# A block of binary convolutions and a mixture of 16 experts on one core: the operands of the up product exchanged, token weights put on the down product, odd pages' down product in float32

## What is computed

```
t = t + ffn(ln_t(t))                               # tokens of 64 values
logits = x @ gate_w + gate_b                       # 16 experts, the best 2 are kept
dispatch = their probabilities, scaled to sum 1
hidden = silu(x @ w1[e]) * (x @ w2[e])             # 64 -> 128 for each chosen expert
out    = sum over chosen e of dispatch[e] * (hidden @ w3[e])   # 128 -> 64
```

## Time and profile before

| | |
|---|---|
| times of three runs | 538.88, 543.08, 543.24 us; median 543.08 |
| span of the profiled execution, first to last instruction | 598.9 us, 14226 instructions |
| TensorE, matmuls | 500.9 us, 84% of the span |
| VectorE | 441.6 us, 74% |
| ScalarE | 396.0 us, 66% |
| GpSimd | 287.9 us, 48% |
| granted TensorE clock, mean | 0.901 |
| chain that ended last | PE 51%, DVE 17%, ACT 10%, issue 9% |

### The profile page before, as it was taken

How to read it: one execution, slowest core, us unless ns; L and a number is a source line. 1 busy time by engine, 2 the same in 40 slices (tenths; PEclk the granted TensorE clock), 3 DMA queues, 4 the chain that set the end, 5 groups by cost and what they waited for, 6 DMA issues and landing times.

```text
span 598.9 us, 14226 instructions
## 1 busy us (share of the span) xinstructions
PE 500.9 (84%) x4186; PEld 436.7 (73%) x4186; DVE 441.6 (74%) x1242; ACT 396.0 (66%) x946; POOL 287.9 (48%) x378
## 2 busy tenths in 40 slices
PE   6899997896986627767889899999999999999854
PEld 5566665674764516757878799999998999899753
DVE  4567786685689697556676688888888888888653
ACT  5577885684765303456676588888787878778650
POOL 4000036666667675645555455454444544545351
PEclk9878997996979557879999899999999999999986
DMA  7941101011000012320122221232242425210404
GB/s 295 283 84 36 35 12 61 25 60 62 25 24 29 22 46 66 69 63 21 39 56 57 54 43 39 51 90 54 48 116 49 118 55 147 55 31 17 134 24 141
DMA packets 62664, 40.97 MB, mean 68 GB/s; under 512 B 50003, under 2 KB 54318, under 8 KB 62080
## 3 DMA queue, kind: packets, MB, share of 16 engines
q1 hardware_dynamic: 52208, 23.84, 17.5%
q0 software_dynamic: 8800, 8.94, 4.4%
q10 hardware_dynamic: 1584, 7.29, 3.2%
HBM read 21.46 MB, written 19.19 MB: 68 GB/s over the span
## 4 chain that ended last, share of the span: by engine, by line
PE 51%; DVE 17%; ACT 10%; issue 9%; another core or an unknown queue 6%; DMA 4%; SPq 3%; POOLq 0%; DVEq 0%; ACTq 0%; POOL 0%
PE up L971 9%; PE up L973 8%; PE turn L987 6%; PE up L803 5%; PE lines L1004 5%; PE small L819 3%; ACT xc L703 3%; DVE hidden L1589 2%; DMA x_in<-in_x 2%; PE lines L1006 2%; PE small L848 2%; PE up L789 2%; PE small L952 2%; PE up L778 2%
## 5 line engine op out<-in xcount | busy, mean ns | idle before, releaser
L519 POOL DMA_INDIRECT results<-result,page_in x147 | 154.3, 1050 | 152.0 <-ACT xc L703 103.5
L498 POOL DMA_INDIRECT pages<-payload,slot_int x128 | 127.6, 997 | 141.7 <-DVE slot_int L1414 73.5
L971 PE MATMUL up<-up_w,xs_hi 128*128 x588 | 163.5, 310 | 9.8 <-issue 5.1
L973 PE MATMUL up<-up_w,xs_lo 128*128 x588 | 150.0, 287 | 0.3 <-issue 0.3
L703 ACT ACTIVATE xc<-up 128x512 f32<-128x512 f32 x147 | 89.5, 609 | 76.5 <-PE up L973 48.4
L971 PEld LDWEIGHTS up<-up_w,xs_hi 128*128 128x128 f32 x588 | 114.1, 194 | 16.2 <-issue 13.7
L973 PEld LDWEIGHTS up<-up_w,xs_lo 128*128 128x128 f32 x588 | 114.7, 195 | 0.0
L1589 DVE SCALAR_TENSOR_TENSOR hidden<-up,page_in,xc 128x128 f32<-128x128 f32 x196 | 59.4, 344 | 43.2 <-ACT xc L703 35.4
L1599 DVE TENSOR_TENSOR hidden_lo<-turn,hidden_hi 128x512 f16<-128x512 f32 x98 | 67.0, 684 | 3.9 <-ACT hidden_hi L716 2.8
L987 PE MATMUL turn<-ident,hidden 128*128 128x128 f32 x392 | 60.7, 279 | 2.8 <-DVE branch L1599 1.6
L716 ACT ACTIVATE hidden_hi<-turn 128x512 f16<-128x512 f32 x98 | 60.9, 622 | 3.1 <-PE turn L987 2.5
(11 more groups left out here) (262 smaller groups left out, 999.2 us busy)
## 6 DMA issues: line engine op xcount, KB each, us to landing
pages<-up_w ACTq DMA_DIRECT2D x4, 1332.0 KB, 9.9
page_in<-pages SPq DMA_DIRECT2D x147, 36.0 KB
page_in<-pages SPq DMA_DIRECT2D x147, 32.0 KB
x_in<-in_x SPq DMA_DIRECT2D x7, 512.0 KB
out<-up_raw SPq DMA_DIRECT2D x5, 512.0 KB, 4.8
results<-result,page_in POOLq DMA_INDIRECT x147
up_raw<-in_L_ffn_w SPq DMA_DIRECT2D x4, 512.0 KB, 16.8
pages<-payload,slot_int POOLq DMA_INDIRECT x128
```

The costliest lines, as they stand in the source:

```text
L498: pool.indirect_dma_start(out=pages, out_offset=bass.IndirectOffsetOnAxis(ap=slot_int[q % PAYLOADS][:, t:t + 1], axis=0), in_=payload[q % ...
L519: pool.indirect_dma_start(out=results, out_offset=bass.IndirectOffsetOnAxis(ap=page_in[g % LOADS][:, k, D + AT_TOKEN:D + AT_TOKEN + 1].bit ...
L971: pe.matmul(target, xs_hi[g % 2][:, k * P:(k + 1) * P], weights[:, bass.ds(e * 2, 2 * HID)], start=True, stop=False)
L973: last = pe.matmul(target, xs_lo[g % 2][:, k * P:(k + 1) * P], weights[:, bass.ds(e * 2, 2 * HID)], start=False, stop=True)
```

## The change

- The up product exchanges its operands: an expert's 128 columns of `up_w` are stationary (gate or value, each apart) and the page's 128 tokens move, `xs_hi` and `xs_lo` one after the other. The result has hidden units in partitions, gates in the first bank and values in the second, each with its own semaphore. `up_w`, `xs_hi` and `xs_lo` are float16, with scales.
- So `turn_hidden` goes. `hide` is one operation on VectorE over all four experts, without the tokens' weights. ScalarE has the silu alone, and `hidden_high` from SBUF for even pages.
- The down product of each expert goes to a place of its own, two pages in one bank of `turn`. Even pages have three float16 matmuls for each expert; odd pages one in float32, from `hidden` and `down_raw`, which is scaled in place.
- VectorE multiplies the down product of two pages by the tokens' weights (`weigh`), and GpSimd sums the four experts of a group in two additions (`sum_up`, called between its scatters by `sums_behind`); for the last two groups VectorE does it (`tail_sum`).
- `LAG` is 3 in place of 4, hidden rows have 4 buffers, and `turn_back` writes to `lines`. `make_hi(0)` and `make_low(0)` move to later steps of the first stage, and the blank page lies in the last three pairs of `x2`.

```diff
-    LAG = 4
-    SCALED = 2
+    LAG = 3
+    RING = 4
...
-        up_w = sb("up_w", [P, E, 2, HID], F32R)
+        up_w = sb("up_w", [P, E, 2, HID], F16)
...
+        def split(n):
+            return n % 2 == 0
...
             def up_product(n, experts):
...
+                at = slice(k * P, (k + 1) * P)
+                for m in range(2):
+                    for j, e in enumerate(experts):
+                        target = up[n % 2][:, m * CW + j * P:m * CW + (j + 1) * P]
+                        own = weights[:, bass.ds(e * (2 * HID // STRIDE) + m * HID, HID)]
+                        pe.matmul(target, own, xs_hi[g % 2][:, at], start=True, stop=False)
+                        last = pe.matmul(target, own, xs_lo[g % 2][:, at], start=False, stop=True)
+                    last.then_inc((gates_ready, up_ready)[m], 1)
...
+            def down_product(n, experts):
+                m, k = n // 2, n % 2
...
                 for j, e in enumerate(experts):
-                    target = up[n % 2][:, 2 * j * HID:2 * (j + 1) * HID]
-                    pe.matmul(target, xs_hi[g % 2][:, k * P:(k + 1) * P], weights[:, bass.ds(e * 2, 2 * HID)],
-                              start=True, stop=False)
-                    last = pe.matmul(target, xs_lo[g % 2][:, k * P:(k + 1) * P], weights[:, bass.ds(e * 2, 2 * HID)],
-                                     start=False, stop=True)
-                last.then_inc(up_ready, 1)
-
-            def turn_hidden(n):
...
+                    target = turn[m % 2][:, (k * PER_LINE + j) * D:(k * PER_LINE + j + 1) * D]
+                    at = slice(j * P, (j + 1) * P)
+                    if split(n):
+                        own_hi = high_low[:, bass.ds(e * 2, D)]
+                        pe.matmul(target, hidden_hi[n // 2 % 2][:, at], own_hi, start=True, stop=False)
+                        pe.matmul(target, hidden_lo[n // 2 % 2][:, at], own_hi, start=False, stop=False)
+                        last = pe.matmul(target, hidden_hi[n // 2 % 2][:, at], high_low[:, bass.ds(e * 2 + D, D)],
+                                         start=False, stop=True)
+                    else:
+                        last = pe.matmul(target, hidden[n % RING][:, at], whole[:, bass.ds(e, D)], start=True, stop=True)
                 last.then_inc(down_done, 1)
...
             def hide(n):
...
+                dve.scalar_tensor_tensor(out=hidden[n % RING], in0=up[n % 2][:, CW:HW], scalar=hidden_scale[:, 0:1],
+                                         in1=act_s[n % 2], op0=ALU.mult, op1=ALU.mult).then_inc(hidden_done, 1)
...
+            def weigh(m):
+                g, k = 2 * m // BY, 2 * m % BY
+                count = min(2, PAGES - 2 * m)
+                dve.wait_ge(down_done, 2 * m + count)
...
+                dve.tensor_tensor(weighed[g % 2][:, k:k + count, :, :], down_pair(m)[:, 0:count, :, :],
+                                  weights.unsqueeze(3).to_broadcast([P, count, PER_LINE, D]), ALU.mult)\
+                    .then_inc(weighed_done, 1)
...
+            def sum_up(g):
+                pool.wait_ge(weighed_done, 2 * g + 2)
...
+                pool.tensor_tensor(halves[:, :, :, :], parts[:, :, 0:2, :], parts[:, :, 2:4, :], ALU.add)\
+                    .then_inc(halved, 1)
+                pool.wait_ge(halved, g + 1)
...
+                pool.tensor_tensor(result[g % LOADS][:, :, :], halves[:, :, 0, :], halves[:, :, 1, :], ALU.add)\
+                    .then_inc(summed, 1)
...
+                if t == PAIRS:
                     make_low(0)
```

More of the change, by code:

```diff
@@ L325, in metaformer_kernel, with down_pair @@
         back_step = {TILES * q + 74 + 2 * c: (q, c) for q in range(EARLY) for c in range(CH)}
-        last_down = {BY * g + pages_of(g) + LAG: g for g in range(GROUPS - 2)}
         LAST = BY * (GROUPS - 2)
[L332 to L336, removed]
+        SUMMED = GROUPS - 2
+        def split(n):
+            return n % 2 == 0
+        def down_pair(m):
+            return turn[m % 2][:, :].rearrange("p (n j d) -> p n j d", n=2, j=PER_LINE)
         @block.sync
@@ L703, in silu @@
-                act.activation(act_s[n % 2].rearrange("p (j h) -> p j h", j=PER_LINE), gates, ACT.Silu)\
+                act.activation(act_s[n % 2], up[n % 2][:, 0:CW], ACT.Silu, scale=gate_unscale[:, 0:1])\
                     .then_inc(silu_done, 1)
[L705 to L709, removed]
@@ L741, in _ @@
+            rows_high(0)
+            for n in range(PAGES + 1):
                 if n < PAGES:
                     silu(n)
-                if n % BY == 2 and n // BY + 1 < GROUPS:
+                if n % BY == 0 and n // BY + 1 < GROUPS:
                     rows_high(n // BY + 1)
+                if n >= 1 and split(n - 1):
+                    hidden_high(n - 1)
             for q in range(EARLY, PAIRS):
@@ L1581, in hide @@
             def hide(n):
[L1582 to L1585 removed]
+                if n >= RING:
+                    dve.wait_ge(down_done, n - RING + 1)
+                dve.wait_ge(up_ready, n + 1)
                 dve.wait_ge(silu_done, n + 1)
[L1587 to L1592 removed]
@@ new lines, in tail_sum @@
+            def tail_sum(m):
+                g, k = 2 * m // BY, 2 * m % BY
+                count = min(2, PAGES - 2 * m)
+                dve.wait_ge(weighed_done, m + 1)
+                if m == 2 * SUMMED:
+                    dve.wait_ge(summed, SUMMED)
+                else:
+                    dve.wait_ge(result_ready, m - 2 * SUMMED)
+                parts = weighed[g % 2][:, k:k + count, :, :]
+                dve.tensor_tensor(halves[:, 0:count, :, :], parts[:, :, 0:2, :], parts[:, :, 2:4, :], ALU.add)\
+                    .then_inc(tail_halved, 1)
+                dve.wait_ge(tail_halved, m - 2 * SUMMED + 1)
```

257 lines of the change are left out of this document (108 added, 149 removed).

## The result

| | before | changed |
|---|---|---|
| median of the runs | 543.16 us (4 runs, 538.88 to 544.23) | 577.16 us (4 runs, 575.18 to 581.97) |
| ratio, with its 95% interval | | 1.065 (1.061 to 1.070) |
| span of the profiled execution | 598.9 us; taken a second time: 540.2 us | 573.1 us |

The change makes the kernel 6.5% slower, 34 us. The forecast was 564 us with a range of 500 to 576: the right side and the right mechanism, and 13 us short.

The account below looks back on a forecast made before the run. The prediction took TensorE to set the pace before (8.21 us per four pages) and its sequencer after (8.8): +22 - 3.4 + 2.4 = +21 us on the median 543.08, giving 564 us, +3.9%, range 500 to 576.

Parts of the forecast that it names:

- The sum for the sequencer: TensorE's sequencer, page stage: address, load and wait instructions of four pages take 8.8 us, against 8.21 a group now.
- I take 8.8, since a recorded step is the row nearest to what the sequencer will do: Page stage: 8.8 us a group chosen over 4.0 from instructions' own times; 36.75 groups give +22 us.
- The transposes back: Ten transposes back into channels leave the bound: 4.7 us on the array before, about 1.3 now, -3.4 us.
- The low half of the first up weight: Moved from second to ninth step of the pair loop, during VectorE's last routing: +2.4 us at most, taken whole.
- The float32 product: Odd page's down product: four float32 matmuls of 64 columns at 0.21 us each, 0.85 us a page.
- the array would no longer bind: TensorE, page stage: a group of four costs the array 6.5 us against 7.6, below the sequencer's 8.8.
- VectorE and ScalarE: Page stage: 6.5 us on VectorE and 4.3 on ScalarE for four pages, both below 8.8, costed at nothing.
- One sign that was named for being right: Steady page stretch: TensorE's matmul busy time per page down by a fifth though the page is no shorter.
- the recorded step is not the sequencer's own: Rival: part of the time around address instructions exists only while profiling; cheaper sequencer, 495 to 535 us, chance 0.36.
- Gain and cost: Rival: gain and cost meet in the page stage, time stays at 538 to 548 us; chance 0.15.
- GpSimd's two additions: Group's sum, about 1.7 us, hidden below 4.6; rival: 2.5 us each gives 579 us, chance 0.05 with the clock.
- The clock: Rival: TensorE, less filled, gets its lower clock a tenth of the time, +15 us, 579; chance 0.05 with GpSimd.

Follow-up runs that it names:

- the last run: Float32 down product on every page, with 55 odd pages' up product as before (tokens stationary), against the changed kernel: 537.2 us, 0.993 of before.

## Why the prediction was wrong by 13 us

**The counts and steps were right.** The sum for the sequencer was 48 FUSED_REGOPS, 8 ALU_OPs, 4 loads and 4 waits for four pages, 8.8 us, with steps read from three starts in the earlier trace rows and three in the earlier trace rows. In the changed kernel the steps from start to start of the sequencer's 1774 instructions between 240 and 500 us, least and median, are 0.124, 0.112 to 0.113, 0.387 to 0.396 and 0.105 to 0.106 us (0.126 for a quarter of the waits); at 0.124, 0.113, 0.395 and 0.11 the sum is 5.95 + 0.90 + 1.58 + 0.44 = 8.87 us.

**The step that failed is "I take 8.8, since a recorded step is the row nearest to what the sequencer will do".** It priced every instruction at its least step. A group of four takes 9.37 us (from 240 to 350 us). The trace has the difference between the sequencer's instructions: about each 1.3 us one step is, most often, 0.02 to 0.15 us longer than its kind's least (391.24 to 391.39 us above is one), together 15.5 of the 280 us from 240 to 520. A sequencer with a third of its time free, as before, catches that up; one that bounds, as here, did not. 0.5 us a group x 36.75 = 18 us, and 0.07 x 36.75 = 3 us for the steps themselves. The same surplus, 5.0 to 5.7% of the time, stands in the runs with float32 on every page, without the low part, and with more waits. Least steps times 1.055 then give a group of four as: changed kernel 9.36 (measured 9.37), float32 everywhere 8.22 (8.21), two more waits 10.25 (10.24), halves everywhere 10.5 (10.54), one load for two pages 7.95 (8.0), one address for two weights 7.3 (7.4 where nothing else is late). The factor was taken from the changed kernel and the first runs, so only the last three test it. What causes these longer steps was not found and stays open; from 240 to 500 us, 190 steps of the changed kernel are more than 0.02 us above their kind's median, 185 without the low part's matmuls and 190 in float32 everywhere with a quarter fewer FUSED_REGOPS, so they go neither with the number of matmuls nor with that of FUSED_REGOPS.

**The transposes back** were to save 3.4 us of 4.7. Before, the five places cost 7.5 us (the second profile), since a pair of them also makes the pages around it wait; the whole stage of before is 9.4 us above 36.5 groups of 8.22, that of the changed kernel 2.7 us above 36.5 groups of 9.37. So some 7 us were gained on irregular pages, most of them these, where 3.4 were entered.

**The low half of the first up weight**, entered at +2.4 us, is not to be seen: the first address of a page stands at 208.3 us against 209.1. It cannot be told apart better, since this start lies anywhere between 207.8 and 218.2 us in the runs of the experiments, whose front part is, but for small edits, one of these two.

**The sum.** 36.5 x (9.37 - 8.22) = +42, -7 for the irregular pages, -2 in front of the stage and behind it: +33, the difference of the two spans. Entered were +22, -3.4 and +2.4. That the forecast came within 13 us is in part luck: it was some 20 us short in the sequencer's sum, and the two entries that were too cautious, with the 2 us outside the stage, gave some 7 of that back. The baseline of 8.21 us, read from a profile that was disturbed elsewhere, held.

**Array, VectorE, ScalarE, GpSimd.** The float32 product, entered at 0.85 us by the nearer of two rows, takes 0.84. That the array would no longer bind is shown by the runs that took matmuls away for nothing and addresses away for 43 us. VectorE and ScalarE are idle for a third and a half of the stage, about as entered. One sign that was named for being right did not come: TensorE's matmul time per page was to fall by a fifth, and it rose from 2.02 us (39.34 us for 19.5 pages) to 2.26 (38.35 for 17). A matmul of the up product is recorded with 0.22 us, so a pair every 0.124 us still counts as an array that is never idle. The Trainium skill's figure for GpSimd's additions (GPSIMD Engine Reference, Performance versus the Vector engine) gave 1.7 us for the two, an estimate by columns; the trace has 2.3.

**The rivals.** That the recorded step is not the sequencer's own fell with the waits: 0.106 us of step, recorded 0.051 of it as the instruction, made 0.105 us of time in each of 292 places. Gain and cost did not meet: the array's queued pairs ran at 0.056 us a matmul. The 81 ns of the Trainium skill (TensorE: Matmul & The Clock Gate, Back-to-back issue gap) appear in no stretch of these runs where work was queued. GpSimd's two additions stayed under their bound, and with the same work on GpSimd the group went to 8.2 and 7.4 us. The clock stayed at 1.00 in the windows of the changed kernel, and at 0.79, in the run without the low part, the page was no longer.

**The range.** Its upper end, 576, was built from the same least steps with little above them. A sum of least steps is a lower bound for the sequencer's part, and the range should have left more room on that side.

## What to carry to other kernels

Count the sequencer's instructions of the busiest engine (addresses, loads of registers, separate waits) as if they were an engine of their own, at the step from start to start rather than at their recorded length, and add some 5% where that sum bounds, as in these runs. Making matmuls smaller or splitting operands multiplies addresses: a matmul that costs the array more but needs one address (float32 here) can be the faster one. Near balance, test each move against both sums; with float32 on every page the array's sum (4 x 1.79 + 0.40 = 7.56 us) lies within 10% of the sequencer's 8.2 us, so that what was taken from the one, in the last run, was lost on the other.

## What the hardware showed beyond what was expected

- On TensorE's sequencer the step to the next instruction of its own is 0.124 us for FUSED_REGOPS (46 ns recorded) and 0.113 for ALU_OP (32 ns), whether one matmul or two stand between, and 0.106 for a met EVENT_SEMAPHORE (51 ns), between which and the next none stands.
- TENSOR_LOAD takes 338 ns for four values and 604 for eight, by these two about 66 ns a value and 70 ns beside them.
- A busy share says little about TensorE here: it is 38 of 40 us busy in the changed kernel, 37 with half of the up product's matmuls left out, and 40.0 where the array bounds.
